# Moving weight sums, one turning load and the last product within the shared-MLP steps of a fused block

## What is computed

```
x = x + tanh(g_xattn[0]) * attention(layernorm(x), ctx_512, ...)
h = layernorm(x)
routed = sum over a token's two experts e of weight * (silu(h @ gate_e) * (h @ up_e)) @ down_e
shared = (silu(h @ gate) * (h @ up)) @ down          # inner width J = 1408
x = x + tanh(g_ffn[0]) * (routed + shared)
```

## Time and profile before

| what | us |
|---|---|
| median of 3 runs | 1918.53 (1915.53 to 1918.86) |
| the profiled execution, its own time | 1905.91 |
| its span in the trace | 1904.1 |
| PE busy in the span | 1845.8 (97%) |
| DVE busy | 1171.1 (62%) |
| ACT busy | 708.6 (37%) |
| POOL busy | 709.9 (37%) |

### The profile page before, as it was taken

How to read it: one execution, slowest core, us unless ns; L and a number is a source line. 1 busy time by engine, 2 the same in 40 slices (tenths; PEclk the granted TensorE clock), 3 DMA queues, 4 the chain that set the end, 5 groups by cost and what they waited for, 6 DMA issues and landing times.

```text
span 1904.1 us, 35031 instructions
## 1 busy us (share of the span) xinstructions
PE 1845.8 (97%) x12962; PEld 1128.1 (59%) x12962; DVE 1171.1 (62%) x2294; ACT 708.6 (37%) x1994; POOL 709.9 (37%) x730
## 2 busy tenths in 40 slices
PE   7799999999999998999999999999998999999998
PEld 7465666666666564444455555555543577777776
DVE  4777777777777776475422222222226788888887
ACT  4656666666666666220122222222211111111111
POOL 4645455555445656100233334343357210110101
PEclk9899999999999999999999999999999999999999
DMA  9456666766666767513299999899944621321202
GB/s 308 118 108 132 131 131 139 147 143 142 137 134 140 167 147 158 147 42 112 76 199 236 239 218 215 221 212 221 209 129 138 111 84 40 95 89 29 84 23 89
DMA packets 478931, 268.47 MB, mean 141 GB/s; under 512 B 410705, under 2 KB 416465, under 8 KB 478801
## 3 DMA queue, kind: packets, MB, share of 16 engines
q1 hardware_dynamic: 467280, 228.90, 51.8%
q0 software_dynamic: 11520, 37.76, 7.5%
HBM read 118.72 MB, written 48.23 MB: 88 GB/s over the span
## 4 chain that ended last, share of the span: by engine, by line
PE 81%; DVE 6%; POOL 4%; ACT 3%; DMA 3%; issue 3%; SPq 1%; DVEq 0%; ACTq 0%; POOLq 0%
PE o L638 13%; PE o L911 8%; PE score L900 7%; PE p_bank L687 7%; PE score L786 6%; PE o L832 5%; PE p_bank L900 4%; PE m_bank L900 4%; PE score L769 3%; PE p_bank L786 3%; PE m_bank L786 3%; PE c_bank L832 3%; PE t_bank L832 3%; DVE arena L1140 2%; PE score L665 2%
## 5 line engine op out<-in xcount | busy, mean ns | idle before, releaser
L638 PE MATMUL o<-arena 128*128 128x512 bf16 x1536 | 352.4, 379 | 1.2 <-DVE arena L1140 1.1
L1140 DVE TENSOR_TENSOR arena<-arena 128x512 bf16<-128x512 f32 (+3 forms) x357 | 300.9, 849 | 17.0 <-ACT arena L1031 4.8
L1586 POOL TENSOR_TENSOR arena<-arena 128x512 f32<-128x512 f32 x128 | 150.6, 1176 | 279.9 <-DVE arena L1161 277.8
L991 ACT ACTIVATE arena<-score,arena 128x128 f32<-128x128 f32 x512 | 181.4, 370 | 160.2 <-DVE arena L1232 160.2
L638 PEld LDWEIGHTS o<-arena 128*128 128x128 bf16 x1536 | 147.7, 98 | 156.5 <-DVE arena L1140 2.0
L687 PE MATMUL p_bank<-arena 128*128 128x256 bf16 x1536 | 181.0, 275 | 1.0 <-DVE arena L1140 0.7
L1678 POOL TENSOR_TENSOR arena<-arena 128x1088 bf16<-128x1088 f32 x32 | 71.9, 2247 | 277.4 <-ACT arena L1021 277.4
L911 PE MATMUL o<-arena 128*128 128x512 bf16 (+1 forms) x720 | 168.5, 380 | 2.0 <-DMA arena<-arena 2.0
L687 PEld LDWEIGHTS p_bank<-arena 128*128 128x128 bf16 x1536 | 146.3, 99 | 25.3 <-DVE arena L1140 1.0
L900 PE MATMUL score<-arena 128*128 128x352 bf16 x960 | 151.5, 315 | 2.9 <-issue 2.9
L786 PE MATMUL score<-arena 128*128 128x256 bf16 x1152 | 144.2, 273 | 4.2 <-DVE arena L1502 4.2
(11 more groups left out here) (210 smaller groups left out, 3222.0 us busy)
## 6 DMA issues: line engine op xcount, KB each, us to landing
xrow_d<-arena SPq DMA_DIRECT2D x80, 256.0 KB, 3.5
arena<-w_expert SPq DMA_DIRECT2D x32, 544.0 KB, 5.1
arena<-w_shared SPq DMA_DIRECT2D x22, 384.0 KB, 3.8
arena<-x SPq DMA_DIRECT2D x16, 512.0 KB, 4.8
arena<-x SPq DMA_DIRECT2D x32, 256.0 KB, 3.4
x_d<-arena SPq DMA_DIRECT2D x32, 256.0 KB, 2.7
xn_d<-arena SPq DMA_DIRECT2D x32, 256.0 KB, 2.4
arena<-x_d SPq DMA_DIRECT2D x8, 1024.0 KB, 7.8
```

The costliest lines, as they stand in the source:

```text
L638: mm = pe.matmul(o_bank[b % 2][:, :], lhsT=cT[u % 2][:, a, h, :], rhs=M_w[:, w, head_of(hg, h), :], start=(hg == 0 and n == 0), stop=(hg = ...
L991: mm = act.activation(prob[:, u % 4, h, :], score_bank[u % 2][:, h * S:(h + 1) * S], ACT.Exp, bias=neg_max[:, u % 4, h:h + 1], accum_out=d ...
L1140: return dve.tensor_tensor(dst, src, hi, ALU.subtract)
L1586: pool.tensor_tensor(prob[:, u % 4], prob[:, u % 4], rden[:, u % 4, :].unsqueeze(2).broadcast_to([P, 4, S]), ALU.mult).then_inc(normed, 1)
```

## The change

Four things are moved within the stage; no arithmetic is added or taken away.

1. Blocks 4 to 10 of the summed weights are spread. `seven_upper` goes from v = 23, 24, 25, 26, 27, 29, 30 to v = 24, 26, 29, 31, 34, 36, 38; POOL's `seven_lower(3)` to `seven_lower(10)`, each with the next block's sums, from v = 23, 24, 25, 26, 27, 29, 30, 31 to v = 23, 25, 27, 30, 33, 35, 37, 39; `load_raw(6)` to `load_raw(10)` from v = 24, 25, 26, 27, 29 to v = 24, 26, 28, 31, 34.
2. Since raw weights are now read later, DVE waits at v = 39, ahead of writing sums of x over them, until all 44 subtractions are done (`w_summed`).
3. `load_xs(4)`, the turning load issued in group 3, goes out at m = 2 (v = 35) instead of m = 0 (v = 33).
4. In the last step of the seven-product kind (v = 87) `down(86)` stands behind product 6 instead of ahead of product 5.

```diff
@@ SP
             def shared_step(v, it):
                 g, m = v // JT, v % JT
-                if v in (24, 25, 26, 27, 29):
-                    load_raw(v - 18 if v < 28 else 10)
+                if v in (24, 26, 28, 31, 34):
+                    load_raw(6 + (24, 26, 28, 31, 34).index(v))
...
-                if m == 0 and 3 <= g < 7:
+                if m == (2 if g == 3 else 0) and 3 <= g < 7:
                     wait(sp, gu_mm, 11 * g, 22, it)
@@ PE, seven(v)
                 product(4, xc[:, :, 0], wc[:, :, 0]).then_inc(product_mm, 1)
-                down(v - 1, None)
+                if v < 8 * JT - 1:
+                    down(v - 1, None)
                 pe.wait_ge(half_done, 7 * n + GATE_A)
                 product(5, x_block(1, 1), wc[:, :, 3]).then_inc(product_mm, 1)
                 pe.wait_ge(half_done, 7 * n + U2)
                 product(6, xc[:, :, 3], w_block(1, 1)).then_inc(gu_mm, 1)
+                if v == 8 * JT - 1:
+                    down(v - 1, None)
@@ ACT
-                if v in (23, 24, 25, 26, 27, 29, 30):
-                    seven_upper(v - 19 if v < 28 else v - 20)
+                if v in (24, 26, 29, 31, 34, 36, 38):
+                    seven_upper(4 + (24, 26, 29, 31, 34, 36, 38).index(v))
@@ DVE, x_combine(g, m)
+                if g == 4 and m == 6:
+                    dve.wait_ge(w_summed, 4 * JT)
                 if m in (6, 9):
@@ POOL
-                if v in (23, 24, 25, 26, 27, 29, 30, 31):
-                    i = v - 20 if v < 28 else v - 21
+                if v in (23, 25, 27, 30, 33, 35, 37, 39):
+                    i = 3 + (23, 25, 27, 30, 33, 35, 37, 39).index(v)
                     seven_lower(i)
                     if i < JT - 1:
                         seven_sums(i + 1)
```

## The result

The changed kernel takes 1903.1 us (median of 1896.96 to 1904.19) against 1918.56 for the kernel before: a ratio of 0.9916, interval 0.9893 to 0.9940, or 15.5 us. A second comparison on another chip gave 1906.07 against 1918.89, a ratio of 0.9939 (0.9919 to 0.9960). The forecast was 1904.9, range 1898 to 1911.

What follows compares the result with a forecast made beforehand. PE is busy 97% of the span, so only its stops and slow stretches can be won. 2.6 + 7.8 + 6.0 + 1.8 - 4.6 = 13.6 us off the median of 1918.53 gives 1904.9, range 1898 to 1911.

Steps and rivals of the forecast that it cites:

- C: PE's 4.21 us stop ahead of product 5 of step 35, and slow matmuls behind: both go, gain 6.0.
- POOL's cost: Last four `seven_lower` and sums of blocks 8 to 10 hold DVE beside steps 33 to 40: costs 4.6.
- signs that were to make it wrong: DVE waiting for `load_xs(4)` at step 37, or rows of six at 1.47 anywhere but behind the stop at `down(87)`.
- A: PE's 2.57 us stop ahead of `down(24)`: goes once the cast stands behind the SiLU, gain 2.6.
- B: PE's 6.43 us stop ahead of `down(29)`, and slow matmuls behind: gather 1 opens earlier, 1.0 left, gain 7.8.
- D: PE's 2.43 us stop ahead of the last `down(87)`: the reordered last step gains 1.8, or 0.5 if PE stays slow.
- Two terms of 1.4 for blocks 8 and 9: Steps 33 to 40: each `seven_lower` holds DVE's last instruction up to 2.13, less 0.74 slack: 1.4 us of stop each.
- The term for block 10: `seven_lower(10)` comes behind gather 3 at another place of the step: half the cost, 0.7 us.
- that for step 33: Sums of block 8 meet the last three DVE instructions of `hidden_seven` at step 33: about 1.1 us.
- The 12.6 us between the profiled execution and the median: Median 1918.53 lies 12.6 above the profiled execution; the same microseconds were taken off it, giving 1904.9.
- at its worst 8.5 for the four `seven_lower`: Upper bound by the skill's rule: each `seven_lower` beside the seven-product steps costs all of its 2.13, 8.5 together.

Runs made afterwards that it cites:

- the changed kernel, again: The changed kernel, unedited, on another chip: 1906.07 against 1918.89 for the kernel before, ratio 0.9939.
- the paced kernel before: Kernel before the change, with gathers 3 to 6 issuing two transfers a step over four steps instead of eight at once: 1904.52 against 1915.12, ratio 0.9941.
- Part 3 alone: Kernel before with only `load_xs(4)` moved from step 33 to step 35: 1916.38 against 1918.89, ratio 0.9989.
- the spread alone: Changed kernel with `load_xs(4)` back at step 33 and the old order of the last step, leaving the spread blocks and their wait: 1907.16, ratio 0.9934.
- the tail alone: Kernel before with only `down(86)` moved behind product 6 of step 87: 1916.84 against 1918.89, ratio 0.9982.
- the paced kernel: Changed kernel with gathers 3 to 6 issuing two transfers a step over four steps instead of eight at once: 1894.66, ratio 0.9872.
- the paced kernel, again: The paced kernel, unedited, on another chip: 1894.89 against 1915.12 for the kernel before, ratio 0.9888.

## Why the prediction was right, point by point

The forecast holds: 15.5 and 12.8 us at the medians of the two comparisons of the changed kernel, 13.6 in the sum. That it comes so near is in part luck, as the points on C, on POOL's cost and on the median show. One of the signs that were to make it wrong appears as well, a row of six at the lower clock level (1.44 at 1541.62 in the changed kernel, again), but behind a wait that the change doesn't bring. The parts, by the table of stretches:

- **A, 2.6.** Right: 24.8 to 22.0, and no stop ahead of `down(24)` in any execution with the spread. What was left open there shows in the paced kernel before: its stop of 2.50 has a row of 2.74 behind it, the lower clock level (granted clock 0.50), where 2.57 in the earlier trace rows has 1.47 (1.00).
- **B, 7.8 with 1.0 left.** Right: 69.2 to 61.2, and 6.6 in the other two pairs. The stop left is 0.73, 1.34 and 1.13, with full speed behind it. The chain is as described: the gather opens 9.0 earlier against step 23 (6.3 to 8.5 was the estimate), lands 13.8 later (13.5), and PE has `hidden(29)` 4.3 after that (4.1).
- **C, 6.0 by part 3.** For the profiled execution the size is right (49.1 in the third stretch, where six steps without stops take 43.1), and the attribution fails. The step that failed is "C goes with its slow stretch", put down to the transposes moving out of gather 2. Part 3 alone does take 5.3 to 5.9 from the stretch, but the spread alone does it too, and the two together no more. The gather opens so much earlier by A and B that it may take its time beside the transposes: 23.00 us of them cost 0.45. The prediction itself said that the gather opens 10 us earlier; the step not taken was to ask whether this alone suffices. With the spread in place part 3 is worth nothing: 1894.90 without it, 1894.89 with it. And C itself is in two of the four executions only; the other two stop at step 33.
- **D, 1.8.** 2.2 in the traces, within the error of the comparison of the tail alone (0.9982, interval 0.9969 to 0.9995: 1.0 to 5.9). DVE's end came as worked out; the stop ahead of the last `down` is 0.40 where it was 2.43, and nothing is slow.
- **POOL's cost, 4.6.** Two terms of 1.4 for blocks 8 and 9: 2.8 measured, by taking `seven_lower` away. The term for block 10 (0.7) and that for step 33 (1.1) were mis-sized: the first is 1.75 in the paced kernel, where L1717 no longer stands behind eight issues of gather 3, and isn't seen in the other, where PE stands still at that moment anyway; for the second the stretch has 2.6, but POOL's sums lengthen one DVE instruction there by 0.4 to 0.5 (L1525, 1.17 for 0.69 in the paced kernel, again; L1527, 0.83 for 0.43 in the profiled execution), and the late start of L1510 comes before them. The mechanism is the one named: L1143 starts 0.42 after L1717 in the profiled execution (1495.08, 1494.66) and takes 2.49 instead of 0.69.
- **The 12.6 us between the profiled execution and the median.** Taken as a shift without a reason, and this was a piece of luck. They are the waits beside gathers 3 to 7, which every traced execution of an unpaced kernel but that one has, with and without the change; so they largely fall out of the difference of the medians. That the untraced executions have them too is inferred, from the median of the paced kernel before. By the two profiled executions alone the change would have seemed worth 8.9, of which only 3.0 lie in the stage that was changed. Without those of gathers 3 to 6 in either kernel it is worth 1904.52 - 1894.89 = 9.6. The difference to 13.6 lies in the third stretch: C's place costs the paced kernel before less (47.6, not 49.1), and `seven_lower(10)` costs the paced kernel after its 1.75.

The rule of the Trainium skill's "SBUF — State Buffer", section "Who interferes with whom", at its worst 8.5 for the four `seven_lower`, is borne out nearly: L1143, the later one, ends 0.55 after L1717 (1497.57 against 1497.02). Held for the whole of L1717 it would end 0.69 after it, its own time, and L1717 would take its 2.13 and not 2.36. What it costs is the part of that hold which exceeds DVE's slack, as the prediction took it: for blocks 8 and 9 2.8 of the 4.3 that two holds of 2.13 would be.

## What to carry to other kernels

Before a difference of two traces is explained, see whether each trace is like the median of its runs: a table of stretches from a row that both kernels have shows in which stretch an execution is not. When two edits can each remove one wait, price them together and not one by one. And where a burst of transfers of one engine stands beside steps that hand over every microsecond, spread it over the steps that have time for it.

## What was not expected of the hardware

Beside the eight indirect transfers of a gather DVE gets PE's signal late: it idles for 3.4 to 3.6 us ahead of L1518, while the product that L1518 reads has long ended (1530.41 + 0.82 = 1531.23 against 1534.96 in the profiled execution after). It is the signal that is late, and not DVE: the trace's record of that semaphore, which stands behind the views, has the rises for this product and the next two of them at 1534.94, 1535.09 and 1535.17, though PE ended these products at 1531.23, 1532.54 and 1533.20. The instruction itself takes its usual 0.42. The Trainium skill says in "SBUF — State Buffer", section "SBUF: two separate sides", that transfers and engines don't slow each other's access; as to how long an instruction takes, the trace agrees with that. This costs 9 to 15 us an execution over gathers 3 to 6 (324.5 to 330.5 in the fourth stretch against 315.7), since PE stops for 1.7 to 2.6 and then again for 0.2 to 0.5, and at times runs at the lower clock level behind it. Two transfers a step instead of eight at once remove it wholly there (315.7 in every paced execution); gather 2, left in one burst, still has it at step 33. Where in the chip the signal is held up the profile doesn't show ("remote" names no engine), and it stays open; the profiled execution of before, with the same bursts, hadn't it.

Each stop costs a little more than the time in its brackets. Since rows overlap by 0.16, a stop adds that much again to PE's busy time. The sums of busy time from step 23 to the end, of before and of after, from the view of stretches (length, PE busy, mean of the ten stretches):

```profile
sum 500.40, PE 481.45; mean PE 48.14
```

```profile
sum 497.40, PE 478.48; mean PE 47.85
```

The slow matmuls behind B, C and D were 2.44 + 1.80 + 1.77 = 6.0 (behind D three rows take 1.93, 1.48 and 1.45 where they take 1.47, 0.81 and 0.81 at full speed), yet busy time fell by only 3.0. The execution after has 19 stops in place of 4, most of them short, and 15 x 0.16 = 2.4 of the missing 3.0.
